# Gate of a mixture-of-experts layer: from steps of two tiles to steps of four

## The chip, the cores and the metric

One core of a Trainium2 chip runs the whole program. The metric is the device time of one execution in microseconds. Engines are called as in the profile: PE is TensorE, DVE VectorE, ACT ScalarE, POOL GpSimd, SP the engine that issues most transfers.

## The reference

A graph network on 6250 nodes of 256 features is followed by a feed-forward layer with eight experts. The change concerns only the second part, cut here to what matters:

```python
H = gelu(xf @ W1 + b1, approximate=False)        # 6250 x 256 -> 6250 x 1024
probs = softmax(H @ Wg + bg)                     # 8 experts
assign = argmax(probs, axis=-1)
for e in range(8):
    y = H @ Wd[e] + bd[e]
    out += where(assign == e, probs[:, e] * y, 0)
out = x + out
```

The result must be close to single precision, so every factor is held as two 16-bit parts, high and low, and a product is made of three or two products of parts.

## The kernel before, in words

The last two stages are `gate` and `experts`, each a block that all engines enter and leave together. A tile is 128 rows (tokens); there are 49, the last one partly filled.

`gate` takes two tiles a step (25 steps, the last with one tile). Its `steps` (L1985) writes steps 0 to 3 out, runs 4 to 21 as nine rounds of a loop of two steps, and writes 22 to 24 out. One step:

- POOL copies the two tiles into `stage` (L2037), a ring of two.
- PE transposes them into one PSUM bank, `TBANK` (L1850, four instructions). The bank is used for every pair, so `pe_transpose` waits (`u.xt`, L1847) until DVE has read the pair before out of it.
- ACT copies the bank to `xt_hi` (L1875), and DVE subtracts that from the bank into `xt_lo` (L1907).
- PE multiplies by `W1` (L1864): the 1024 hidden columns are eight chunks of 128, and a chunk takes six products with 256 columns (two tiles) into one of four PSUM banks.
- For each chunk ACT applies gelu (`hf`, L1893). For five chunks of eight ACT also makes the high part `h_hi` (L1888), for chunks 1, 4 and 6 DVE does (L1920). DVE makes the low part `h_lo` of all (L1925). `hf` holds all eight chunks of a step.
- PE makes the gate's logits from `h_hi` and `h_lo` (`logits`, L2057, 16 products of 16 columns per tile), one step later.
- DVE chooses the expert of every token (`choose`, L2119 to L2139, nine small instructions in a chain, two steps later); PE counts the rank of each token within its expert (`ranks`, L2066 to L2071); DVE turns rank into a place in `sorted_rows` (`place`, L2141 to L2153, five small instructions in a chain, four steps later); POOL scatters the rows there (L2042), one indirect transfer per tile, six steps after their staging.

The order on each engine is the order of the code. Of a two-tile step DVE runs `place` behind the `h_lo` of chunk 0, and behind the `h_lo` of chunk 3 first `xt_lo` of the next step and then `choose`. PE transposes the next two tiles behind chunk 1, counts ranks behind chunk 4, and makes the logits of the step before behind chunk 7:

```python
between[1] = lambda: transpose(i + 1, 1 - par, nxt)
between[4] = lambda: ranks(pe, i - 3, 1 - par, 2, n)
pe_hidden(pe, m, u, i, par, 1 if n == NPAIR else 2, between)
logits(pe, i - 1, 1 - par, 2)
```

After the last `place`, DVE computes the table of tiles for `experts` (L2171 to L2200). SP loads the down weights `wd` and the bias table `bd` (L2000, L2002) at the start of `gate`. `experts` takes 28 pairs of sorted tiles through the same hidden products (`pe_hidden`, `act_hidden`, `dve_hidden`), multiplies by the expert's `wd` (L2276) and scatters the rows to `out`. SP issues its row loads (L2230) one pair after the other, four pairs ahead.

Of the kernel before, what the change touches and what calls it, by code (L numbers as in the profile page):

```python
# [1797 lines left out]
def ffn(nc, m, a):  # L1798
    m.wd = m.at("wd", m.wd_at, [P, NEXP, KH // 2, 2, 2, C], F16)
    take = Place(m, m.ff_at + 8192)  # L1800
    m.xt_hi, m.xt_lo = take("xt_hi", [P, 2, KC, 2 * P], F16), take("xt_lo", [P, 2, KC, 2 * P], F16)
    m.hf = take("hf", [P, KH, 2 * P], F32)
    m.h_hi, m.h_lo = take("h16_hi", [P, 2, KH, 2 * P], F16), take("h16_lo", [P, 2, KH, 2 * P], F16)
    assert take.next <= m.ring_at
    m.hidden = hidden_semaphores(m, "hid")
    gate(nc, m, a)
    experts(nc, m, a)
# [6 lines left out]
UB = 4  # L1814
DVE_HIGH = (1, 4, 6)
# [134 lines left out]
def gate(nc, m, a):  # L1950
# [6 lines left out]
    lg, mx = take("lg", [P, NT + 1, NEXP], F32), take("mx", [P, 2], F32)  # L1957
    now = take("now", [P, 2, NEXP], F32)
    sc, best = take("sc", [P, 2, NEXP], F32), take("best", [P, 2], F32)
    oh, ohf = take("oh", [P, 2, 2, NEXP], F16), take("ohf", [P, 2, 2, NEXP], F32)  # L1960
    rk, slotf, slot = take("rk", [P, 2, NEXP], F32), take("slotf", [P, 2], F32), take("slot", [P, NT], I32)
# [7 lines left out]
    tq, tw = (m.hf[0:1, 2 * q:2 * q + 2, :].rearrange("a k n -> a (k n)").rearrange("a (e t) -> a e t", t=64) for q in range(2))  # L1969
    m.probs = take("probs", [P, NT], F32)  # L1970
    m.bd = m.at("bdB", m.ring_at, [P, NEXP, C], F32)
    u = m.hidden
# [6 lines left out]
    m.s_bd, m.s_prob = S("j_bd"), s_store  # L1979
    m.s_wd = S("i_wd")  # L1980
    NPAIR = NT // 2
    LB, RB = (5, 7), 6
    tiles = lambda i: 1 if i == NPAIR else 2

    def steps(eng, step):  # L1985

        for i in range(4):
            step(eng, i, i % 2, i)
        with eng.Fori(2, NPAIR // 2 - 1) as k:
            step(eng, 2 * k, 0, None)  # L1990
            step(eng, 2 * k + 1, 1, None)
        for i in range(NPAIR - 2, NPAIR + 1):
            step(eng, i, i % 2, i)

    with nc.Block() as block:
        @block.sync
        def _(sp):
            for e in range(0, NEXP, 2):
                n = KH // 2
                sp.dma_start(m.wd[:, e:e + 2, :, :, :, :].rearrange("p e k h t c -> p (e k) (h t c)"),  # L2000
                             m.wd_dram[e * n:(e + 2) * n, :, :].rearrange("n p f -> p n f")).then_inc(m.s_wd, 16)
            sp.dma_start(m.bd[:, :, :].rearrange("p e c -> p (e c)"), bass.AP(a.fbd.tensor, 0, [[0, P], [1, NEXP * C]])).then_inc(m.s_bd, 16)  # L2002
            sp.wait_ge(s_const, 8)
            sp.dma_start(m.sorted_rows[NEXP * REG:NEXP * REG + P, :], prow[:, :]).then_inc(s_padded, 16)
            sp.wait_ge(s_pads, 1)
            for e in range(NEXP):
                at = sp.value_load(padi[0:1, e:e + 1], min_val=e * REG, max_val=e * REG + NP_)
                sp.dma_start(m.sorted_rows[bass.ds(at, P), :], prow[:, :]).then_inc(s_padded, 16)
            sp.wait_ge(s_probS, 1)
            sp.dma_start(m.prob_dram.rearrange("(t p) c -> t (p c)", p=P), probT[:, :]).then_inc(m.s_prob, 16)  # L2010
            sp.wait_ge(s_padded, 16 * (NEXP + 1))

        @block.gpsimd
        def _(pool):
# [16 lines left out]
            LATE = 6  # L2031
            for i in range(NPAIR + 1 + LATE):
                if i <= NPAIR:
                    n = tiles(i)
                    if i >= 2:
                        pool.wait_ge(u.tr, i - 1)
                    pool.tensor_copy(stage[:, i % 2, 0:n, :], rows[:, 2 * i:2 * i + n, 0:C]).then_inc(s_stage, 1)  # L2037
                if i >= LATE:
                    pool.wait_ge(s_slot, i - LATE + 1)
                    for t in range(2 * (i - LATE), 2 * (i - LATE) + tiles(i - LATE)):  # L2040
# [6 lines left out]
        def _(pe):  # L2047
            pe_ahead(pe, u)
            pe.wait_ge(s_const, 8)

            def logits(pe, i, par, ntile):
                pe.wait_ge(u.split, i * KH + 2 * KH)
                pe.wait_ge(s_lgfree, i + 1)
                for j in range(ntile):
                    for n, h in enumerate((m.h_hi, m.h_lo)):
# [17 lines left out]

            def transpose(i, par, ntile):
                pe.wait_ge(s_stage, i + 1)
                pe_transpose(pe, m, u, i, lambda j, k: stage[:, par, j, k * P:(k + 1) * P], ntile)

            def step(pe, i, par, n):
                nxt = 0 if n == NPAIR else 1 if n == NPAIR - 1 else 2

                between = {}
                if nxt:
                    between[1] = lambda: transpose(i + 1, 1 - par, nxt)
                if n is None or n >= 3:
# [14 lines left out]
        def _(act):  # L2099
            act.sem_inc(u.gelu, UB)  # L2100
            act_xt(act, m, u, 0, 0, 2)

            def step(act, i, par, n):
                nxt = 0 if n == NPAIR else 1 if n == NPAIR - 1 else 2
                act_hidden(act, m, u, i, par, 1 if n == NPAIR else 2, nxt)
            steps(act, step)
            act.wait_ge(s_oh, NPAIR + 1)
            act.activation(lg[:, 0:NT, :], lg[:, 0:NT, :], ACT.Exp).then_inc(s_ex, 1)

        @block.vector  # L2110
        def _(dve):
            link = chain_on(m, dve)
            dve_ahead(dve, u)
            dve.sem_inc(s_lgfree, 2)
            link(dve.memset(ones16[:, :], 1.0))
            dve.wait_ge(s_const, 8)

            def choose(dve, i, par, ntile):
# [14 lines left out]
                dve.tensor_copy(lg[:, bass.ds(2 * i, ntile), :], l)  # L2133
# [7 lines left out]
            def place(dve, i, par, ntile):  # L2141
# [9 lines left out]
                lk(dve.tensor_tensor(run[:, :], run[:, :], m.ps[:, RB, 2 * NEXP:3 * NEXP], ALU.add), 3)  # L2151
                lk(dve.tensor_reduce(slotf[:, t], rk[:, t, :], AX.X, ALU.add), 4)
                dve.tensor_copy(slot[:, bass.ds(2 * i, ntile)], slotf[:, t]).then_inc(s_slot, 1)  # L2153

            def step(dve, i, par, n):
                nxt = 0 if n == NPAIR else 1 if n == NPAIR - 1 else 2

                between = {}
                if n is None or n >= 4:
                    between[0] = lambda: place(dve, i - 4, par, 2)  # L2160
                if n is None or n >= 2:
                    between[3] = lambda: choose(dve, i - 2, par, 2)
                dve_hidden(dve, m, u, i, par, 1 if n == NPAIR else 2, nxt, between)
            dve_xt(dve, m, u, 0, 0, 2)
            steps(dve, step)
            for i in range(NPAIR - 3, NPAIR + 1):
                place(dve, i, i % 2, tiles(i))
                if i < NPAIR - 1:
                    choose(dve, i + 2, i % 2, tiles(i + 2))
# [27 lines left out]
            link(dve.tensor_reduce(m.probs[:, :], lg[:, 0:NT, :], AX.X, ALU.add))  # L2197
# [5 lines left out]
def experts(nc, m, a):  # L2203
# [6 lines left out]
    bd = m.bd  # L2210
    y = take("y", [P, 2, 2, C], F32)
    assert take.next <= m.ff_at
    u = m.hidden
    u.first = -(-NT // 2)
    S = m.sem
    s_bd, s_y, s_out, s_used = m.s_bd, S("j_y"), S("j_out"), S("j_used")
# [7 lines left out]
    with nc.Block() as block:  # L2224
        @block.sync
        def _(sp):
# [34 lines left out]
        def _(pe):  # L2261
            def transpose(i, par, q, uses):
# [37 lines left out]
        def _(act):  # L2300
# [7 lines left out]

            act_xt(act, m, u, 0, 0, 2)
# [11 lines left out]
        def _(dve):  # L2321
            dve.sem_inc(s_y, 2)
            dve.sem_inc(s_out, 2)
            dve.wait_ge(s_bd, 16)
# [16 lines left out]
            dve_hidden(dve, m, u, 0, 0, 2, 2)  # L2341
            with dve.Fori(0, (NPAIR - 2) // 2) as k:
# [33 lines left out]
```

## Time and profile before

| | us |
|---|---|
| median of 3 runs | 1857.0 (1855.56 to 1859.79) |
| the profiled execution, its own time | 1859.56 |
| its span | 1857.8 |
| `gate`: first transpose to last slot | 1298.57 to 1511.61 |
| `experts`: first transpose to the end | 1528.68 to 1857.8 |

Over the span PE is busy 85%, DVE 63%, ACT 52%, POOL 50%; the granted clock of PE is 0.97 of full speed on average. These are averages over stages with different limits; `gate` is some 11% of the span. In a timeline row the first number is the start, the second the time from the first start to the last end of merged instructions, `x` their count, and brackets give the engine's idle time before and what ended it.

### The profile page before, as it was taken

What the parts mean: (1) busy time and instruction counts of PE and PEld (TensorE: products, weight loads), DVE (VectorE), ACT (ScalarE), POOL (GpSimd) and SP (SyncE); (2) the same over time, 40 slices, a digit from 0 to 9 for tenths busy, and PEclk for the clock granted to TensorE, in tenths of its full rate; (3) what the DMA queues carried; (4) which work ended last, traced back from release to release, by engine and by line L of the source; (5) the groups of instructions that cost most, each with busy time, mean ns of one, the idle gap of its engine ahead of it and who ended that gap; (6) DMA issues with size and microseconds to landing.
All of it is one profiled execution on the core that took longest, in us unless ns stands there. A gap on an engine that the chain in (4) does not pass through costs nothing. (4 is left out here: it accounts for less than half of the span.)

```text
span 1857.8 us, 36775 instructions
## 1 busy us (share of the span) xinstructions
PE 1579.0 (85%) x11153; PEld 1182.1 (64%) x11154; DVE 1178.6 (63%) x4511; ACT 971.2 (52%) x2001; POOL 936.2 (50%) x989
## 2 busy tenths in 40 slices
PE   0229999999999896989999999975888839999996
PEld 0215666666666696856656555655777728899995
DVE  6478888888886377932234344337788965656663
ACT  0555555555554355832334222228888837766773
POOL 5747677777777000047777777723133332333433
PEclk9999999999999897999999999989999969999998
DMA  8546566666666000478999999837500021111110
GB/s 248 164 138 214 193 208 208 209 208 208 209 208 208 12 0 32 148 260 309 299 314 313 336 321 313 291 122 231 195 34 34 32 75 33 48 47 46 48 47 15
DMA packets 152562, 305.72 MB, mean 165 GB/s; under 512 B 26099, under 2 KB 107989, under 8 KB 144638
## 3 DMA queue, kind: packets, MB, share of 16 engines
q1 hardware_dynamic: 104354, 191.99, 29.6%
q0 software_dynamic: 41744, 105.90, 18.1%
q10 hardware_dynamic: 6348, 6.40, 1.1%
q8 instruction: 58, 0.95, 0.2%
q14 instruction: 58, 0.48, 0.1%
HBM read 212.02 MB, written 99.68 MB: 168 GB/s over the span
## 5 line engine op out<-in xcount | busy, mean ns | idle before, releaser
L1165 POOL DMA_INDIRECT grows<-table_dram,gsrc x680 | 657.9, 967 | 337.3 <-issue 309.0
L1099 PE MATMUL ps<-table,adj 128*128 128x512 f16 x2842 | 707.1, 381 | 5.7 <-PEq L1466 5.7
L1099 PEld LDWEIGHTS ps<-table,adj 128*128 128x128 f16 x2842 | 389.7, 142 | 169.3 <-issue 12.1
L856 ACT ACTIVATE adj<-ps 128x490 f16<-128x490 f32 (+1 forms) x390 | 223.5, 573 | 182.3 <-PE ps L841 178.2
L1893 ACT ACTIVATE hf<-ps,b1f,unscale 128x256 f32<-128x256 f32 (+1 forms) x424 | 233.4, 562 | 119.6 <-PE ps L1864 95.8
L1864 PE MATMUL ps<-xt_hi,fw_parts 128*128 128x256 f16 (+1 forms) x1696 | 255.4, 274 | 5.5 <-DVE xt_lo L1907 5.3
L828 DVE TENSOR_SCALAR oh_k<-iota_k,keyrem 128x246 f16<-128x246 f16 x780 | 237.8, 309 | 0.0
L1925 DVE SCALAR_TENSOR_TENSOR h_lo<-hf,beta,h_hi 128x256 f16<-128x256 f32 (+1 forms) x424 | 190.1, 482 | 70.0 <-ACT h_hi L1888 64.3
L827 DVE TENSOR_SCALAR oh_r<-iota_r,keyrem 128x128 f16<-128x128 f16 x780 | 214.9, 278 | 26.6 <-PE ps L841 21.6
L1048 PE MATMUL ps<-grows,oh_g 128*128 128x512 f16 x680 | 167.1, 380 | 18.0 <-DMA grows<-table_dram,gsrc 18.0
L1864 PEld LDWEIGHTS ps<-xt_hi,fw_parts 128*128 128x128 f16 x1696 | 162.4, 98 | 26.2 <-DVE xt_lo L1907 5.4
L841 PE MATMUL ps<-oh_k,oh_r 128*128 128x245 f16 x780 | 148.7, 273 | 17.3 <-DVE oh_k L828 13.6
L1864 PE MATMUL ps<-xt_lo,fw_parts 128*128 128x256 f16 (+1 forms) x848 | 162.3, 273 | 0.0
L2276 PE MATMUL ps<-wd,h_hi 128*128 x896 | 148.4, 273 | 0.9 <-DVE y L2333 0.9
L841 PEld LDWEIGHTS ps<-oh_k,oh_r 128*128 128x128 f16 x780 | 75.6, 98 | 94.8 <-DVE oh_k L828 20.2
L1888 ACT ACTIVATE h_hi<-hf,beta 128x256 f16<-128x256 f32 (+1 forms) x265 | 133.0, 502 | 1.7
L920 DVE SCALAR_TENSOR_TENSOR tmp_d<-ps,disP,tmp_d 128x256 f32<-128x256 f32 x30 | 14.5, 484 | 186.6 <-ACT tmp_d L1124 186.6
L913 DVE TENSOR_SCALAR oh_g<-iota_r,gloc 128x128 f16<-128x128 f16 x680 | 125.7, 281 | 0.3
L1048 PEld LDWEIGHTS ps<-grows,oh_g 128*128 128x128 f16 x680 | 65.4, 98 | 93.3 <-DMA grows<-table_dram,gsrc 23.9
L2255 POOL DMA_INDIRECT out<-out_rows,in_rows x56 | 57.3, 1023 | 130.3 <-DVE out_rows L2337 121.8
L2276 PE MATMUL ps<-wd,h_lo 128*128 x448 | 122.1, 273 | 0.0
L2042 POOL DMA_INDIRECT sorted_rows<-rows,slot x49 | 48.5, 989 | 128.6 <-DVE slot L2153 121.0
(354 smaller groups left out, 2228.8 us busy)
## 6 DMA issues: line engine op xcount, KB each, us to landing
adj_dram<-adj SPq DMA_DIRECT2D x30, 1568.0 KB
adj<-adj_dram SPq DMA_DIRECT2D x30, 1568.0 KB, 8.2
cv_raw<-fwd SPq DMA_DIRECT2D x64, 256.0 KB, 5.5
table_dram<-table SPq DMA_DIRECT2D x14, 896.0 KB, 4.1
grows<-table_dram,gsrc POOLq DMA_INDIRECT x680
wd_dram<-cv_parts SPq DMA_DIRECT2D x32, 256.0 KB, 5.1
wd<-wd_dram SPq DMA_DIRECT2D x4, 2048.0 KB, 16.8
in_rows<-sorted_rows SPq DMA_DIRECT2D x56, 129.5 KB, 2.1
```

The source lines that it names most:

```text
L827: dve.tensor_scalar(a.oh_r[:, n % OHR, i, :], m.iota_r[:, :], m.keyrem[:, 1, j, w:w + 1], None, ALU.is_equal)
L828: last = dve.tensor_scalar(a.oh_k[:, n % OHR, i, :], m.iota_k[:, :], m.keyrem[:, 0, j, w:w + 1], None, ALU.is_equal)
L841: last = pe.matmul(m.ps[:, n % 3, at:at + keys], a.oh_r[:, n % OHR, i, :], a.oh_k[:, n % OHR, i, 0:keys], start=True, stop=True)
L856: act.activation(m.adj[:, q % 3, d0:d0 + wide, :].rearrange("r d c -> r (d c)"), m.ps[:, n % 3, 0:wide * NT], ACT.Copy).then_inc(a.s_adj, 1)
L1048: last = pe.matmul(acc, m.oh_g[:, n % GOR, j, :], m.grows[:, n % GR, j, :], start=False, stop=part == PT - 1 and j == PARTS[part] - 1)
L1099: last = pe.matmul(acc, adj[:, :, c], table[:, c, :], start=c == 0, stop=c == NT - 1)
L1165: pool.indirect_dma_start(m.grows[:, n % GR, j, :], None, m.table_dram, bass.IndirectOffsetOnAxis(ap=m.gsrc[:, g, part * BT + j:part * BT ...
L1864: last = pe.matmul(m.ps[:, h % UB, 0:n], m.w1[:, 2 * k + half, w, at:at + P], x[:, par, k, 0:n], start=q == 0 and k == 0, stop=q == 2 and ...
L1888: act.activation(m.h_hi[:, par, h, 0:n], m.hf[:, h, 0:n], ACT.Copy, scale=m.beta[:, h:h + 1]).then_inc(u.hi, 1)
L1893: act.activation(m.hf[:, h, 0:n], m.ps[:, h % UB, 0:n], ACT.Gelu, bias=m.b1f[:, h:h + 1], scale=m.unscale[:, 0:1]).then_inc(u.gelu, 1)
L1925: dve.scalar_tensor_tensor(m.h_lo[:, par, h, 0:n], m.hf[:, h, 0:n], m.beta[:, h:h + 1], m.h_hi[:, par, h, 0:n], ALU.mult, ALU.subtract).th ...
L2276: last = pe.matmul(m.ps[:, DB + j, 0:C], h[:, par, k, j * P:(j + 1) * P], w, start=q == 0 and k == 0, stop=q == 2 and k == KH - 1)
```

## The change

`gate` takes four tiles a step (`QT = 4`), 13 steps, the last with one tile: steps 0 to 3 are written out, 4 to 9 are three rounds of a loop of two, 10 to 12 are written out. The hidden products, gelu, `h_hi` and `h_lo` are 512 columns wide. `hf` becomes a ring of four chunks (`HFR = 4`), and gelu of chunk h waits for the `h_lo` of chunk h-4. `choose`, `ranks` and `place` work on four tiles; `ranks` of four tiles takes 14 products. Transposing stays in pairs through the one bank `TBANK`: two pairs for the next step, one behind chunk 1, one behind chunk 4 on PE; ACT and DVE read them behind chunks 2 and 5. On DVE `place` stands behind chunk 0, now for three steps before, and `choose` behind chunk 1, for two steps before. `ranks` stands behind chunk 7, before `logits`. POOL scatters eight pairs after staging (before: six). `experts` keeps its pairs and gets its own buffers and semaphores; the load of `bd` moves from the start of `gate` to `experts`, behind the loads of the first pair of rows.

```diff
+QT, HFR = 4, 4
...
-            sp.dma_start(m.bd[:, :, :].rearrange("p e c -> p (e c)"), bass.AP(a.fbd.tensor, 0, [[0, P], [1, NEXP * C]])).then_inc(m.s_bd, 16)
...
-            LATE = 6
+            LATE = 8
...
+            def transpose(p, par, ntile):
+                pe.wait_ge(s_stage, p + 1)
+                pe.wait_ge(u.xt, p + 1)
+                for j in range(ntile):
+                    for k in range(KC):
+                        last = pe.transpose(m.ps[:, TBANK, k * 2 * P + j * P:k * 2 * P + (j + 1) * P],
+                                            stage[:, par, j, k * P:(k + 1) * P], m.id32[:, :])
+                last.then_inc(u.tr, 1)
+
+            def hidden(i, par, n, between):
+                wide = (QT if n is None else tiles(n)) * P
+                for h in range(KH):
+                    if h == 0:
+                        pe.wait_ge(u.xt, i * 2 + (3 if n is None else 1 + -(-tiles(n) // 2)))
+                    pe.wait_ge(u.gelu, i * KH + (h + 1))
...
+                            last = pe.matmul(m.ps[:, h % UB, 0:wide], m.w1[:, 2 * k + half, w, at:at + P], x[:, par, k, 0:wide],
+                                             start=q == 0 and k == 0, stop=q == 2 and k == KC - 1)
...
             def step(pe, i, par, n):
                 between = {}
+                for half in range(to_come(n)):
+                    ntile = 2 if n is None else min(2, tiles(n + 1) - 2 * half)
+                    between[1 + 3 * half] = lambda half=half, ntile=ntile: transpose(2 * i + (2 + half), half, ntile)
+                hidden(i, par, n, between)
+                if n is None or n >= 2:
+                    ranks(i - 2, par, QT, n)
                 if n is None or n >= 1:
+                    logits(i - 1, 1 - par, QT)
...
+                    act.wait_ge(u.up, i * KH + (h + 1 + 2 * KH))
+                    act.wait_ge(u.split, i * KH + (h + 1))
...
+                    if h in (2, 5) and (h - 2) // 3 < to_come(n):
+                        half = (h - 2) // 3
+                        xt_low(2 * i + (2 + half), 1 - par, half, 2 if n is None else min(2, tiles(n + 1) - 2 * half))
+                    if h == 0 and (n is None or n >= 3):
+                        place(dve, i - 3, 1 - par, QT)
+                    if h == 1 and (n is None or n >= 2):
+                        choose(dve, i - 2, par, QT)
...
             for i in range(RB4):
                 load(i, i)
+                if i == 0:
+                    sp.dma_start(bd[:, :, :].rearrange("p e c -> p (e c)"), bass.AP(a.fbd.tensor, 0, [[0, P], [1, NEXP * C]])).then_inc(s_bd, 16)
```

DVE before, in the written-out step 3 (`h_lo` of chunks 1 to 3, the lowering of the next pair, `choose` of step 1, chunk 4's `h_hi`; `place` joins from step 4 on):

```order
L1925 SCALAR_TENSOR_TENSOR h_lo<-hf,beta,h_hi 128x256 x3
L1907 TENSOR_TENSOR xt_lo<-ps,xt_hi 128x512
L2128 SCALAR_TENSOR_TENSOR now<-ps,inv_g,bgB 128x16
L2129 SCALAR_TENSOR_TENSOR now<-ps,inv_g,now 128x16
L2130 TENSOR_REDUCE mx<-now 128x2
L2131 TENSOR_TENSOR now<-now,mx 128x16
L2133 COPY lg<-now 128x16
L2134 SCALAR_TENSOR_TENSOR sc<-now,prio 128x16
L2135 TENSOR_REDUCE best<-sc 128x2
L2136 TENSOR_TENSOR ohf<-sc,best 128x16
L2139 CAST oh<-ohf 128x16
L1920 TENSOR_SCALAR h_hi<-hf,beta 128x256
```

DVE now, in the written-out step 3 (the first row is `h_lo` of chunk 1; `place` stands ahead of it, behind chunk 0):

```order
L2229 SCALAR_TENSOR_TENSOR q_h_lo<-q_hf,beta,q_h_hi 128x512
L2191 SCALAR_TENSOR_TENSOR now<-ps,inv_g,bgB 128x32
L2192 SCALAR_TENSOR_TENSOR now<-ps,inv_g,now 128x32
L2193 TENSOR_REDUCE mx<-now 128x4
L2194 TENSOR_TENSOR now<-now,mx 128x32
L2196 COPY lg<-now 128x32
L2197 SCALAR_TENSOR_TENSOR sc<-now,prio 128x32
L2198 TENSOR_REDUCE best<-sc 128x4
L2199 TENSOR_TENSOR ohf<-sc,best 128x32
L2202 CAST oh<-ohf 128x32
L2229 SCALAR_TENSOR_TENSOR q_h_lo<-q_hf,beta,q_h_hi 128x512
L2177 TENSOR_TENSOR q_xt_lo<-ps,q_xt_hi 128x2x256
```

The lowering of the transposed rows, which stood ahead of `choose`, now stands behind it.

PE now, in the same step (`stage` rows are the transposes, one pair each; the three pairs of rows between are chunks 2 to 4):

```order
L2065 MATMUL ps<-id_66,stage 128x128 x4
L2078 MATMUL ps<-q_xt_hi,fw_parts 128x512 x4
L2078 MATMUL ps<-q_xt_lo,fw_parts 128x512 x2
L2078 MATMUL ps<-q_xt_hi,fw_parts 128x512 x4
L2078 MATMUL ps<-q_xt_lo,fw_parts 128x512 x2
L2078 MATMUL ps<-q_xt_hi,fw_parts 128x512 x4
L2078 MATMUL ps<-q_xt_lo,fw_parts 128x512 x2
L2065 MATMUL ps<-id_66,stage 128x128 x4
```

Before, one set of transposes stood in a step of eight chunks; now there are two, three chunks apart.

SP now, at the start of `experts`:

```order
L2310 DMA in_rows<-sorted_rows 128x259
L2315 DMA bdB<-fbd 128x2048
L2309 TENSOR_LOAD tile_row
L2309 ISA x2
L2310 ISA
L2310 DMA in_rows<-sorted_rows 128x259
```

The load of `bd` stands between the rows of the first pair and those of the second.

## Rows read from the trace of the kernel before

**Rows 1.** Stretches: busy us of each engine, its count, PE's clock, DMA

```profile
core 0: us, PE busy (x) PEld busy (x) DVE busy (x) ACT busy (x) POOL busy (x), PEclk, DMA share, GB/s
1400.00:1425.00 25.00, 21.24 (x276) 18.70 (x275) 22.26 (x80) 21.18 (x44) 7.73 (x9) 1.00 0.09 32
1600.00:1625.00 25.00, 25.00 (x231) 22.50 (x230) 15.83 (x38) 18.41 (x40) 9.36 (x10) 1.00 0.17 51
```

**Rows 2.** Waits in 1330 to 1480: us in total, times, longest us

```profile
PE ps L2066 <- DVE slot L2153: 24.8, 18, 1.9
```

**Rows 3.** Timeline of PE, 1394 to 1412

```profile
1394.48 0.17 PE L2066 MATMUL ps<-oh,tri 128*128 128x8 f16 x1 [1.54 <-DVE slot L2153]
...
1402.65 0.60 PE L1864 MATMUL ps<-xt_hi,fw_parts 128*128 128x256 f16 x4
...
1404.61 0.35 PE L2057 MATMUL ps<-wg,h_hi 128*128 128x16 f16 x8
...
1405.42 0.60 PE L1864 MATMUL ps<-xt_hi,fw_parts 128*128 128x256 f16 x4
...
1410.84 0.17 PE L2066 MATMUL ps<-oh,tri 128*128 128x8 f16 x1 [1.54 <-DVE slot L2153]
```

**Rows 4.** Timeline of DVE, 1402 to 1412

```profile
1402.41 0.35 DVE L1920 TENSOR_SCALAR h_hi<-hf,beta 128x256 f16<-128x256 f32 x1
1402.80 1.28 DVE L1925 SCALAR_TENSOR_TENSOR h_lo<-hf,beta,h_hi 128x256 f16<-128x256 f32 x3
1403.99 0.68 DVE L1907 TENSOR_TENSOR xt_lo<-ps,xt_hi 128x512 f16<-128x512 f32 x1
1404.59 0.23 DVE L2128 SCALAR_TENSOR_TENSOR now<-ps,inv_g,bgB 128x16 f32<-128x16 f32 x1
...
1406.83 0.35 DVE L1920 TENSOR_SCALAR h_hi<-hf,beta 128x256 f16<-128x256 f32 x1
...
1409.60 0.17 DVE L2148 TENSOR_TENSOR rk<-ps,run 128x16 f32<-128x16 f32 x1
...
1410.64 0.35 DVE L1920 TENSOR_SCALAR h_hi<-hf,beta 128x256 f16<-128x256 f32 x1
```

**Rows 5.** Groups by form of ACT, whole span: busy us, mean ns

```profile
L1893 ACT ACTIVATE hf<-ps,b1f,unscale 128x256 f32<-128x256 f32 x416 | 230.1, 564 | 117.9 <-PE ps L1864 94.0 <-DVE h_lo L1925 9.4
...
L1667 ACT ACTIVATE agg<-agg,b2c,a 128x512 f32<-128x512 f32 x24 | 17.8, 799 | 6.4 <-DVE b2c L1612 6.4
...
L778 ACT ACTIVATE cv_parts<-cv_raw,w_scale 128x512 f16<-128x512 f32 x4 | 2.6, 709 | 0.0
```

**Rows 6.** Groups by form of DVE, whole span

```profile
L796 DVE SCALAR_TENSOR_TENSOR cv_parts<-cv_raw,w_scale,cv_parts 128x512 f16<-128x512 f32 x4 | 2.8, 748 | 2.4 <-ACT cv_parts L778 2.4
```

**Rows 7.** Timeline of PE in the aggregation stage

```profile
1213.46 7.29 PE L1099 MATMUL ps<-table,adj 128*128 128x512 f16 x33
```

**Rows 8.** Timeline of PE around two waits for a transfer

```profile
968.24 1.92 PE L1048 MATMUL ps<-grows,oh_g 128*128 128x512 f16 x5 [2.16 <-DMA grows<-table_dram,gsrc]
969.95 2.95 PE L1099 MATMUL ps<-table,adj 128*128 128x512 f16 x8
...
1027.74 1.47 PE L1048 MATMUL ps<-grows,oh_g 128*128 128x512 f16 x6 [2.78 <-DMA grows<-table_dram,gsrc]
```

**Rows 9.** Stretch behind the first of these waits, columns as in rows 1

```profile
968.00:972.00 4.00, 3.76 (x10) 1.49 (x11) 2.09 (x6) 2.93 (x6) 3.09 (x4) 0.58 0.64 174
```

**Rows 10.** Timeline of PE at the start of the gate

```profile
1298.57 1.09 PE L1850 MATMUL ps<-id,stage 128*128 128x128 f32 x4 [9.68 <-POOL stage L2037]
...
1301.17 1.04 PE L1864 MATMUL ps<-xt_hi,fw_parts 128*128 128x256 f16 x4 [1.52 <-DVE xt_lo L1907]
```

**Rows 11.** Timeline of SP: start of the gate, start of the experts

```profile
1307.56 5.35 SPq L2002 DMA_DIRECT2D bdB<-fbd  x1
...
1525.26 4.95 SPq L2230 DMA_DIRECT2D in_rows<-sorted_rows  x5
```

**Rows 12.** Timeline of PE at the start of the experts

```profile
1533.83 1.06 PE L1850 MATMUL ps<-id,in_rows 128*128 128x128 f32 x4
```

More of the change, by code:

```diff
@@ L1799, in ffn @@
     m.wd = m.at("wd", m.wd_at, [P, NEXP, KH // 2, 2, 2, C], F16)
[L1800 to L1805, printed above, removed]
     gate(nc, m, a)
@@ L1968, in gate @@
     tb2 = take("tb2", [1, NEXP], F32)
-    tq, tw = (m.hf[0:1, 2 * q:2 * q + 2, :].rearrange("a k n -> a (k n)").rearrange("a (e t) -> a e t", t=64) for q in range(2))
     m.probs = take("probs", [P, NT], F32)
-    m.bd = m.at("bdB", m.ring_at, [P, NEXP, C], F32)
-    u = m.hidden
+    take = Place(m, m.ff_at + 8192)
+    xt_hi, xt_lo = take("q_xt_hi", [P, 2, KC, QT * P], F16), take("q_xt_lo", [P, 2, KC, QT * P], F16)
+    hf = take("q_hf", [P, HFR, QT * P], F32)
+    h_hi, h_lo = take("q_h16_hi", [P, 2, KH, QT * P], F16), take("q_h16_lo", [P, 2, KH, QT * P], F16)
+    assert take.next <= m.ring_at + 24576
+    tq, tw = (hf[0:1, q, :].rearrange("a (e t) -> a e t", t=64) for q in range(2))
+    u = hidden_semaphores(m, "quad")
     S = m.sem
@@ L2095, in _ @@
+            for i in range(NQ - 2, NQ):
+                ranks(i, i % 2, tiles(i), i)
             pe.wait_ge(s_prob, 1)
@@ L2155, in step @@
             def step(dve, i, par, n):
[L2156 to L2164, printed above, removed]
+                wide = (QT if n is None else tiles(n)) * P
@@ new lines, in step @@
+                highs = 0
+                for h in range(KH):
+                    if h in DVE_HIGH:
+                        dve.wait_ge(u.gelu, i * KH + (h + 1 + UB))
+                        dve.tensor_scalar(h_hi[:, par, h, 0:wide], hf[:, h % HFR, 0:wide], m.beta[:, h:h + 1], None, ALU.mult).then_inc(u.own, 1)
+                        dve.wait_ge(u.own, i * len(DVE_HIGH) + (DVE_HIGH.index(h) + 1))
+                    else:
+                        highs += 1
+                        dve.wait_ge(u.hi, i * (KH - len(DVE_HIGH)) + highs)
+                    dve.scalar_tensor_tensor(h_lo[:, par, h, 0:wide], hf[:, h % HFR, 0:wide], m.beta[:, h:h + 1], h_hi[:, par, h, 0:wide],
+                                             ALU.mult, ALU.subtract).then_inc(u.split, 1)
+                    if h in (2, 5) and (h - 2) // 3 < to_come(n):
+                        half = (h - 2) // 3
+                        xt_low(2 * i + (2 + half), 1 - par, half, 2 if n is None else min(2, tiles(n + 1) - 2 * half))
[3 more added lines that the diff above has]
+                        choose(dve, i - 2, par, QT)
@@ L2165, in _ @@
+            for half in range(2):
+                xt_low(half, 0, half, 2)
             steps(dve, step)
[L2166 to L2169, printed above, removed]
+            for i in range(NQ - 2, NQ):
+                choose(dve, i, i % 2, tiles(i))
+                place(dve, i - 1, (i - 1) % 2, tiles(i - 1))
+            place(dve, NQ - 1, (NQ - 1) % 2, tiles(NQ - 1))
@@ L2209, in experts @@
     pr = take("prob_rows", [P, 2, 2, 1], F32)
-    bd = m.bd
     y = take("y", [P, 2, 2, C], F32)
     assert take.next <= m.ff_at
-    u = m.hidden
-    u.first = -(-NT // 2)
+    take = Place(m, m.ff_at + 8192)
+    m.xt_hi, m.xt_lo = take("xt_hi", [P, 2, KC, 2 * P], F16), take("xt_lo", [P, 2, KC, 2 * P], F16)
+    m.hf = take("hf", [P, KH, 2 * P], F32)
+    m.h_hi, m.h_lo = take("h16_hi", [P, 2, KH, 2 * P], F16), take("h16_lo", [P, 2, KH, 2 * P], F16)
+    bd = take("bdB", [P, NEXP, C], F32)
+    assert take.next <= m.ring_at + 24576
+    u = hidden_semaphores(m, "hid")
     S = m.sem
-    s_bd, s_y, s_out, s_used = m.s_bd, S("j_y"), S("j_out"), S("j_used")
+    s_bd, s_y, s_out, s_used = S("j_bd"), S("j_y"), S("j_out"), S("j_used")
     s_row = [S(f"j_row{q}") for q in range(RB4)]
```

133 lines of the change are left out of this document (82 added, 51 removed).

## The prediction

> **What bounds the kernel now.** I first read the page's slices to find the stage. The gate runs from 1298.6 to 1511.6 and is all that the change touches, but for one transfer. The table of stretches comes next: in the middle of the gate DVE is busy 22.3 us of 25, PE 21.2, ACT 21.2; in the experts PE is busy without a break [rows 1]. Shares so close say little, so I read who waits for whom: PE waits in each of 18 steps for DVE's `slot`, 24.8 us in all [rows 2], and the first rank product comes back every 16.36 us per two steps, that is per four tiles [rows 3]. That is DVE's own work: from start to start `h_lo` takes 0.40 (three in 1.19), `h_hi` 0.39, `xt_lo` 0.60, `choose` 2.24, `place` 1.04 [rows 4]. For four tiles: 16×0.40 + 6×0.39 + 2×0.60 + 2×2.24 + 2×1.04 = 16.5. So DVE bounds the gate, and PE has 1.5 us of idle time in a step.
>
> **The change, engine by engine, for four tiles.** DVE: a 512-wide instruction of `h_lo`'s form takes 748 ns [rows 6], the 256-wide one 0.48 (1.28 less two starts of 0.40) [rows 4], so from start to start 0.40 + 0.27 = 0.67. For a 512-wide `h_hi` no row stands; between 0.39 (no more than now) and 0.66 (growing like `h_lo`) I take the middle, 0.53. `choose` and `place` are chains of small instructions whose price is not their width: 2.24 and 1.04 come once instead of twice, with some 0.1 for 16 more columns each: 2.35 and 1.10. Sum: 8×0.67 + 3×0.53 + 2×0.60 + 2.35 + 1.10 = 11.6, that is 4.9 less.
> PE: 27 products of 512 columns take 7.29 - 1.47 us [rows 7, 8], 0.216 each, a chunk of six 1.30. Three chunks of 256 columns take 1404.61 - 1402.65 = 1.96 now [rows 3], 0.65 each. So width saves PE nothing: 10.4 for eight chunks. Logits: 0.81 for two tiles [rows 3], 1.62 for four, 0.025 a product; 14 rank products 0.36; transposes are 128 columns wide, 8×0.11 = 0.9. Sum 13.3.
> ACT: gelu 0.56 now; a 512-wide activation takes 0.80, and one of `h_hi`'s form 0.71 [rows 5]. With some 0.1 of overlap between neighbours: 8×0.70 + 5×0.61 + 2×0.5 = 9.7.
> POOL: the same 49 scatters; the second pair's staging now stands behind two scatters that wait for `place`, but it is still done about 1 us before PE can use it (2.5 for two scatters and 0.6 for the copy, behind `place`, against `choose`, two `h_lo`, one `h_hi` and `xt_lo`, 4.9 with what is below).
> If these sums decided, a step would cost PE's 13.3. They don't, for a loop runs through all three engines.
>
> **The loop.** There is one bank for transposing, and PE may fill it for the second pair (behind chunk 4) only when DVE has lowered the first pair out of it (behind chunk 2). DVE comes there only after `place` and `choose`; before, the lowering stood ahead of `choose`, and the next transposing a whole step later. Follow it from the moment the second transposing starts:
> PE: transposes 0.44, chunks 5 to 7 3.90, ranks 0.36, logits 1.62, chunks 0 and 1 of the next step 2.60: 8.9.
> Handover to ACT (the last product's end, 0.16, and the signal, 0.1): 0.3.
> ACT: `h_hi` of chunk 0 stands behind gelu of chunk 1: 0.70 + 0.71: 1.4.
> DVE: `h_lo` 0.67, `place` 1.10, `h_hi` 0.53, `h_lo` 0.67, `choose` 2.35, `h_lo` 0.67, `xt_lo` 0.68: 6.7; signal 0.1.
> Sum 17.4 us against 16.36 now. PE's wait at its second transposing is 17.4 - 13.3 = 4.1. A step of four tiles costs 1.0 more, though every engine has less or the same to do. It holds for steps 4 to 10: 7×1.0 = **+7**.
>
> **The clock.** Behind an idle time of 2.16 us PE was granted 1.2 GHz: the mean of the next 4 us is 0.58 [rows 9], and 5 and 8 products took 1.92 and 2.95 us [rows 8], where full speed gives 4×0.216+0.39 = 1.25 and 1.90: 1.7 us lost. Behind 2.78 at 1027.74 six products took 1.47, full speed [rows 8]; so between 2.2 and 2.8 it happens or not, and the 1.5 us of the gate now leave 1.00 [rows 1, 3]. A wait of 4.1 is longer than any after which the clock held. The cost per step lies between 0 (it holds) and 3.9 (chunks 5 to 7 wholly at half speed); I take 1.4, somewhat under the 1.7 measured, since a part of the slow stretch can fall into the wait or onto the small products. The chunks behind the wait are on the loop, so it counts whole, in steps 3 to 10: 8×1.4 = **+11**.
> The Trainium skill has the same on its page "TensorE: Matmul & The Clock Gate", section "Why this matters for your kernels": it advises against idle gaps between bursts of products, as they bring the half clock back. By that rule the clock falls in each such step; by the shorter waits of this trace alone it could hold, and the second rival is what is left then. This rule speaks against the change.
>
> **Start, end, `bd`.** At the start the second pair must go through the bank before the first product: one more round of 2.6 us, as from 1298.57 to 1301.17 [rows 10]. In steps 0 to 3 DVE has little or no `choose` and `place` and the wait is short; there the saved DVE time can give this back. I take 0 for both, between -4 and +4. At the end the chain of `choose` and `place` behind the last tile is of fewer pieces: **-2**, between -3 and 0. SP needs 5.35 us to issue `bd` [rows 11]; in the gate nothing waited behind it, now the second pair's row loads do. SP issues rows about 1 us apart from 1525.3 (five in 4.95), so the fourth lands, some 2 us behind its issue, at about 1530.6; with `bd` ahead at 1536. PE wants them at 1533.83 [rows 12], so 2 us late; PE is the bound of the experts [rows 1] and doesn't catch up. Between 0 and 5 with the clock's share, I take **+3**. DVE's wait for `bd` is moved behind the first hidden step and covered.
>
> **Sum:** 7 + 11 + 0 - 2 + 3 = +19 on the profiled execution's 1859.56: 1878.6. That execution lies 2.6 above the median of the runs (1857.0), against which +19 gives 1876. I say **1877**. Own range 1869 to 1886.
>
> **Rivals.**
> 1. *DVE's saving arrives* (faster). The gate is bound by DVE now and loses 4.9 us of it per four tiles, so a step falls to PE's 13.3: 12×(16.36 - 13.3) = 37 less, +3 for `bd`, 1823. The point that decides is whether the first pair is lowered within the 4.3 us that PE needs from chunk 1 to its second transposing (0.44 + 3×1.30); by my loop it takes 8.4. For: rows 2 and 4. Against: the order of the code. Were the path a good 1 us shorter than I say and the clock to hold, the result would be near 1857. The Trainium skill favours this rival on "VectorE: DVE Perf Modes", section on the TRN2 errata: it advises wide tiles since each instruction pays a fixed price. The trace agrees with that for DVE alone (0.67 against 2×0.40), not for the gate by itself. Chance 0.12.
> 2. *The loop binds, the clock holds*: 19 less 11, 1865 to 1868. For: 2.78 us without a fall. Chance 0.18.
> 3. *Worse than that*: all three chunks behind the wait are slow in most steps, 8×3 instead of 8×1.4: 1890. Against: the measured 1.7. Chance 0.12.
> 4. *The terms cancel*, 1857 within 4. Chance 0.04.
> My forecast keeps 0.54. That the change doesn't widen the work is excluded by the order of instructions, which shows 128x512 on all three engines.
>
> **Numbers.** 0.2% of this time, about 3.7 us, is what a measurement can tell from no change. Slower: 0.54 + 0.18 + 0.12 = 0.84; same 0.04; faster 0.12. The range 1860 to 1890 holds the forecast, rival 2 and the lower half of rival 3, about 0.8.
>
> **What would show it.** In the profile of the changed kernel: a wait of about 4 us of PE at the second transposes for DVE's `xt_lo`, once per step; PE's clock under 1.00 in the gate, about 0.8 to 0.9, with products of a chunk behind the wait about twice as slow; a period of 18 to 19 us per step; DVE busy less than 70% of the gate; second transposes of the experts some 2 us later behind the start than 5.2. I am wrong if PE is busy throughout the gate, if its wait is under 3 us, if the clock stays 1.00, or if another wait (ACT's for the ring of `hf`, PE's for ranks or logits) is the long one.

## The result and the profile after

| | us |
|---|---|
| before, median of 4 runs | 1857.2 (1855.56 to 1859.79) |
| changed, median of 4 runs | 1893.2 (1888.94 to 1895.41) |
| ratio, 95% interval | 1.0183 (1.0165 to 1.0202) |
| profiled execution of the changed kernel, and its span | 1895.41, 1893.5 |
| `gate`: first transpose to last slot | 1302.07 to 1542.77 |
| `experts`: first transpose to the end | 1564.76 to 1893.5 |

The change costs 36 us, where 19 were forecast; 1893 is outside the range of 1860 to 1890. The stretches that answer to [rows 1], with the same columns:

```profile
core 0: us, PE busy (x) PEld busy (x) DVE busy (x) ACT busy (x) POOL busy (x), PEclk, DMA share, GB/s
1400.00:1425.00 25.00, 16.71 (x138) 9.20 (x139) 15.97 (x39) 11.09 (x17) 9.55 (x11) 0.81 0.11 38
1600.00:1625.00 25.00, 25.00 (x231) 22.55 (x230) 15.61 (x38) 18.01 (x39) 9.79 (x10) 1.00 0.15 44
```

The experts are as before. In the gate no engine is busy for more than some two thirds of the stretch, and PE's clock, 1.00 before, is 0.81. The waits of 1345 to 1480 (us in total, times, longest), which answer to [rows 2], have the pair of names that the forecast's loop asked for:

```profile
ACT q_hf L2149 <- PE ps L2078: 57.1, 29, 6.7
DVE q_h_lo L2229 <- ACT q_h_hi L2144: 50.0, 14, 5.0
PE ps L2065 <- DVE q_xt_lo L2177: 28.4, 7, 4.4
ACT q_hf L2149 <- DVE q_h_lo L2229: 7.2, 4, 1.8
```

Each engine waits for the one before it round the loop: ACT for PE, DVE for ACT, PE for DVE. The ring of four `hf` is the last line: 7.2 us against the 57.1 that ACT waits for PE. PE's timeline over one step, which answers to [rows 3]:

```profile
1424.32 1.09 PE L2065 MATMUL ps<-id,stage 128*128 128x128 f32 x4 [4.41 <-DVE q_xt_lo L2177]
1425.19 1.91 PE L2078 MATMUL ps<-q_xt_hi,fw_parts 128*128 128x512 f16 x4
1426.90 1.06 PE L2078 MATMUL ps<-q_xt_lo,fw_parts 128*128 128x512 f16 x2
...
1429.86 1.03 PE L2078 MATMUL ps<-q_xt_hi,fw_parts 128*128 128x512 f16 x4
1430.73 0.59 PE L2078 MATMUL ps<-q_xt_lo,fw_parts 128*128 128x512 f16 x2
...
1444.62 1.09 PE L2065 MATMUL ps<-id,stage 128*128 128x128 f32 x4 [4.41 <-DVE q_xt_lo L2177]
```

A step takes 20.3 us. Behind the wait of 4.41 four products take 1.91 us; in the last chunk they take 1.03. The stretches of one step show the same in the clock, 1.2 GHz for 6.8 us, 2.4 GHz for 13.6:

```profile
1422.40:1429.20 6.80, 4.88 (x14) 2.37 (x15) 4.07 (x8) 1.12 (x2) 2.79 (x3) 0.51 0.11 39
1429.20:1442.80 13.60, 11.00 (x122) 6.06 (x119) 7.84 (x21) 9.03 (x14) 2.83 (x4) 0.99 0.05 20
```

**Where the 35.7 us of span went**, by the starts of the same transposes in both traces:

| stretch | before | changed | difference |
|---|---|---|---|
| up to the gate's first transpose | 1298.6 | 1302.1 | +3.5 |
| from there to the transposing of pair 10 | 75.4 | 73.4 | -2.0 |
| from there to pair 24 (seven steps) | 114.3 | 141.9 | +27.7 |
| from there to the last slot | 23.3 | 25.4 | +2.0 |
| last slot to the experts' first transpose | 17.1 | 22.0 | +4.9 |
| experts | 329.1 | 328.7 | -0.4 |

The first line is code that the change doesn't touch; in a second profile of the changed kernel (below) the gate began at 1299.6, so it is scatter between executions. The other lines are the change. Seven steps cost 4.0 us more each, where 2.4 were forecast (1.0 for the loop, 1.4 for the clock), and 4.9 us lie behind the gate, where the forecast had a gain. The experiments ask three things: is it this loop, is the clock's part an effect of the idle time, and what is late behind the gate.

### The profile page after: what moved, and what is told of

Same layout as the page of the kernel before. It is cut to its first block and busy times, and to the rows that moved or that the text cites. A ratio compares the mean times of both kernels' runs of the same rounds, so it can differ in the third digit from the quotient of the medians.

```text
span 1893.5 us, 34507 instructions
## 1 busy us (share of the span) xinstructions
PE 1596.6 (84%) x10625; PEld 1136.3 (60%) x10626; DVE 1142.1 (60%) x4211; ACT 930.2 (49%) x1845; POOL 941.4 (50%) x989
## 5 line engine op out<-in xcount | busy, mean ns | idle before, releaser
L1888 ACT ACTIVATE hf<-ps,b1f,unscale 128x256 f32<-128x256 f32 x224 | 123.0, 565 | 87.5 <-PE ps L1859 80.1
L841 PE MATMUL ps<-oh_k,oh_r 128*128 128x245 f16 x780 | 148.6, 273 | 17.4 <-DVE oh_k L828 13.7
L1920 DVE SCALAR_TENSOR_TENSOR h_lo<-hf,beta,h_hi 128x256 f16<-128x256 f32 x224 | 103.8, 484 | 58.7 <-ACT h_hi L1883 55.6
L1859 PE MATMUL ps<-xt_hi,fw_parts 128*128 128x256 f16 x896 | 136.2, 275 | 2.4 <-DVE xt_lo L1902 2.4
L841 PEld LDWEIGHTS ps<-oh_k,oh_r 128*128 128x128 f16 x780 | 75.6, 98 | 94.9 <-DVE oh_k L828 20.3
L2149 ACT ACTIVATE q_hf<-ps,b1f,unscale 128x512 f32<-128x512 f32 (+1 forms) x104 | 78.1, 752 | 100.9 <-PE ps L2078 89.9
L2229 DVE SCALAR_TENSOR_TENSOR q_h_lo<-q_hf,beta,q_h_hi 128x512 f16<-128x512 f32 (+1 forms) x104 | 75.1, 735 | 85.5 <-ACT q_h_hi L2144 84.2
L2078 PE MATMUL ps<-q_xt_hi,fw_parts 128*128 128x512 f16 (+1 forms) x416 | 115.0, 404 | 3.1 <-DVE q_xt_lo L2177 3.0
```

Of the source, the lines that this page charges most:

```text
L841: last = pe.matmul(m.ps[:, n % 3, at:at + keys], a.oh_r[:, n % OHR, i, :], a.oh_k[:, n % OHR, i, 0:keys], start=True, stop=True)
L1859: last = pe.matmul(m.ps[:, h % UB, 0:n], m.w1[:, 2 * k + half, w, at:at + P], x[:, par, k, 0:n], start=q == 0 and k == 0, stop=q == 2 and ...
L1888: act.activation(m.hf[:, h, 0:n], m.ps[:, h % UB, 0:n], ACT.Gelu, bias=m.b1f[:, h:h + 1], scale=m.unscale[:, 0:1]).then_inc(u.gelu, 1)
L2078: last = pe.matmul(m.ps[:, h % UB, 0:wide], m.w1[:, 2 * k + half, w, at:at + P], x[:, par, k, 0:wide], start=q == 0 and k == 0, stop=q == ...
```

## The experiments

### Is it the one bank and DVE's order?

`e1_choose_behind` puts `choose` behind the lowering of the first pair. POOL's `LATE` goes to 10 with it, so that staging stands ahead of the scatters that wait for `place`:

```diff
-            LATE = 8
+            LATE = 10
...
-                    if h == 1 and (n is None or n >= 2):
+                    if h == 2 and (n is None or n >= 2):
                         choose(dve, i - 2, par, QT)
```

> The changed kernel with choose on DVE behind the first pair's xt_lo (chunk 2) instead of ahead of it (chunk 1), and POOL's scatters two pairs later (LATE 10) so that the second pair's staging doesn't stand behind the scatters of the same step. Theory (one bank for transposing, filled again only when DVE has lowered the first pair): the loop loses choose's 2.5 us, PE's wait at the second transposing falls from 4.4 to about 1.7, the clock then holds 1.00 in the gate as it did with 1.5 us of idle time before, and a step goes from 20.4 to about 15.0: 8 x 5.4 = 43 less, about 1850. Rival ring (the ring of four hf buffers sets the step): DVE's work is the same and so is the step, 1893. Rival clock alone (the order of DVE's work is worth its 2.5 us, the clock falls anyway): 8 x 2.5 = 20 less, 1873.

Measured: 1854.9 against 1861.2 of before on that chip, ratio 0.9955 (0.994 to 0.997); on the first chip's 1857 that is 1849. PE's waits in 1395 to 1475:

```profile
PE ps L2065 <- DVE q_xt_lo L2177: 8.6, 5, 1.7
```

A step takes 15.2 us (four from 1391.30 to 1452.21), the clock is 1.00 throughout. `LATE` has a share in this that the theory didn't see (shown below); beside the kernel with `LATE` 10 alone, 1880.5 on the same chip, moving `choose` gives 26 us. Both rivals fall, the ring among them: DVE has the same work and ACT the same ring.

`e2_two_banks` leaves DVE's order and gives each half a bank of its own; `choose`'s logits give one up. `LATE` is 10 here too; the lines that only follow from the new banks are left out:

```diff
-    LB, RB = (5, 7), 6
+    LB, RB, TB = (7, 7), 6, (TBANK, 5)
...
-                pe.wait_ge(u.xt, p + 1)
+                pe.wait_ge(u.xt, max(p, 1) if isinstance(p, int) else p)
...
-                pe.wait_ge(s_lgfree, i + 1)
+                pe.wait_ge(s_lgfree, i + 2)
```

> The changed kernel with a bank of its own for each half of the transposing (both steps' logits share one bank in its place), DVE's order untouched, LATE 10 as above. Theory: PE no longer waits at the second transposing; a step is bound by PE's own 13.3 to 14.1 us at full clock: 8 x 6.3 = 50 less, and the first product comes 2.6 us sooner: about 1840. Rival (DVE arrives late whatever the banks are): the wait moves to the next step's chunk 0 and the step stays over 17: above 1870. Rival ring: 1893.

Measured: 1847.5 against 1861.2, ratio 0.9924 (0.9908 to 0.9941). The second transposing never waits. A wait of 1.1 to 1.25 us came at the next step's chunk 0 for the second pair's `xt_lo`:

```profile
1377.23 1.03 PE L2078 MATMUL ps<-q_xt_hi,fw_parts 128*128 128x512 f16 x4 [1.25 <-DVE q_xt_lo L2177]
```

Steps are by turns 14.4 and 16.3 us, since the clock falls in every other one. Beside `LATE` 10 alone that is 33 us less. So the loop through the one bank is the cause: the wait shrinks to 1.7 us by DVE's order alone and is gone with a second bank. The step of 14.1 wasn't reached, as the rival's late lowering is there too, at a smaller price.

### LATE alone: a surprise

`e4_late10` has the one line `LATE = 10` and was meant as a control.

> The changed kernel with LATE 10 instead of 8 alone, the control for the two kernels that have it too. Theory: in the changed kernel the second pair's staging is ready before PE can use it, so nothing changes: 1893 within 3, wait at the second transposing 4.4 as before. Rival (the staging behind two scatters is what PE waits for): the wait falls by 1 us or more, 8 us or more less.

Measured: 1880.5 against 1861.2, ratio 1.0103 (1.0086 to 1.012). The expectation was wrong: 0.8% of time, some 15 us, hangs on when POOL copies a pair. The rival was nearer in its number, but not in its mechanism: in the changed kernel the copy (1441.78, 0.62 us) ends 2.2 us ahead of the transposes that need it (1444.62). DVE in the changed kernel:

```profile
1441.14 0.66 DVE L2194 TENSOR_TENSOR now<-now,mx 128x32 f32<-128x32 f32 x1
1442.06 0.39 DVE L2196 COPY lg<-now 128x32 f32 x1 [0.26 <-DVE now L2194]
```

and POOL in the same step:

```profile
1440.81 0.97 POOL L2050 DMA_INDIRECT sorted_rows<-rows,slot  x1 [0.30 <-issue]
1441.78 0.62 POOL L2045 COPY stage<-rows 128x512 f32<-128x512 f32 x1
```

With `LATE` 10 a scatter runs there too, but the next copy begins 3.2 us or more behind the subtraction, and DVE's timeline has:

```profile
1417.32 0.19 DVE L2194 TENSOR_TENSOR now<-now,mx 128x32 f32<-128x32 f32 x1
1417.76 0.18 DVE L2196 COPY lg<-now 128x32 f32 x1 [0.25 <-DVE now L2194]
```

In four traces (the changed kernel twice, the two-bank kernel, the best one below) the subtraction takes 0.59 to 0.68 in the 26 steps in which the copy follows directly behind a scatter and begins as the subtraction ends, and 0.19 in all others. The copy by itself doesn't do it. In `e1_choose_behind` it begins in the last 0.05 us of the subtraction in eight steps, but 0.60 us behind the scatter, and the subtraction takes 0.19 in all eight:

```profile
1407.16 0.19 DVE L2194 TENSOR_TENSOR now<-now,mx 128x32 f32<-128x32 f32 x1
1407.30 0.61 POOL L2045 COPY stage<-rows 128x512 f32<-128x512 f32 x1 [0.60 <-PE ps L2065]
```

So the place of the copy is shown as the cause of the longer `choose`, and why it has to stand right behind a scatter isn't. With the longer copy of `lg` (0.39 for 0.18) it makes 0.67 us in the middle of the loop: from the start of the subtraction to DVE's next `h_lo` are 1.98 us against 1.31. PE's wait falls from 4.41 to 3.74, and behind that the clock falls for one stretch of 3.4 us, if at all, instead of 6.8: steps take 17.1 (1383.99 to 1401.13) to 19.0, 18.25 in the mean. The Trainium skill says on "SBUF — State Buffer", section "SBUF: two separate sides", that VectorE and GpSimd share a pair of ports that one of them locks for a whole instruction. The trace agrees that the two disturb each other; which of them held the lock it doesn't show.

### Is the clock's part due to the idle time?

`e3_fill` gives PE 20 products to make while it waits:

```diff
+                    if h == 4 and (n is None or n >= 3) and 4 in between:
+                        pe.wait_ge(u.gelu, i * KH + 6)
+                        for _ in range(20):
+                            pe.matmul(m.ps[:, 5 % UB, 0:512], m.w1[:, 0, 0, 0:P], xt_hi[:, par, 0, 0:512], start=True, stop=True)
                     if h in between:
```

> The changed kernel with 20 extra products of 512 columns (4.3 us at full clock; their result is overwritten by chunk 5) on PE just ahead of the second transposing, in the time in which it waited 4.4 us. Nothing else moves. Theory (the idle time is what drops the clock): granted clock 1.00 in the middle of the gate, the loop alone is left, a step of about 17.9 instead of 20.4: 8 x 2.5 = 20 less, 1873. Rival (the clock falls for another reason, or it costs nothing since the loop hides it): the clock still shows 0.67 and the time is 1893 or up to 20 more, since slow filling products take 8.6 us.

Measured: 1875.1 against 1861.2, ratio 1.0079 (1.0061 to 1.0096): 1.0% or 19 us under the changed kernel's 1.0183, for more work. Its PE:

```profile
1411.78 4.48 PE L2084 MATMUL ps<-q_xt_hi,fw_parts 128*128 128x512 f16 x20
1416.36 0.63 PE L2065 MATMUL ps<-id,stage 128*128 128x128 f32 x4
1416.82 1.03 PE L2078 MATMUL ps<-q_xt_hi,fw_parts 128*128 128x512 f16 x4
```

The clock is 1.00 from 1347 to 1514, and a step takes 17.8 us. The filling ends just ahead of `xt_lo` (DVE's row is 1415.53, 0.69 us), so the loop still sets the step. That splits the 20.3: 16.3 before, 1.5 for the loop, 2.5 for the clock. The idle time brings the clock down, and its price is on the path.

`e8_fill10` is the same with 10 products.

> The changed kernel with 10 filling products (2.15 us at full clock) instead of 20 ahead of the second transposing: an idle time of about 2.3 us is left. In the changed kernel 1.66 us never brought the clock down and 2.51 did once, for 3.4 us. Theory (the length of the idle time decides, in steps): the clock falls in some steps for 3.4 us, a step between 17.8 and 19, 1875 to 1885. Rival (any idle time of over 2 us costs the whole): 20.4 a step, 1893. Rival (only over 3): as with 20 products, 1875.

It ran on a chip on which every kernel was slow (before took 2125.8, 14% more; in the traces of the changed kernels from there nearly all of that lies ahead of the gate). Measured: 2154.6, ratio 1.0135 (1.0109 to 1.0162). Its gate keeps the engines' usual speeds and can be read. The same idle time, two steps in a row:

```profile
1673.25 0.63 PE L2065 MATMUL ps<-id,stage 128*128 128x128 f32 x4 [2.25 <-DVE q_xt_lo L2181]
1673.71 1.03 PE L2078 MATMUL ps<-q_xt_hi,fw_parts 128*128 128x512 f16 x4
...
1691.21 0.63 PE L2065 MATMUL ps<-id,stage 128*128 128x128 f32 x4 [2.25 <-DVE q_xt_lo L2181]
1691.68 1.51 PE L2078 MATMUL ps<-q_xt_hi,fw_parts 128*128 128x512 f16 x4
```

With 2.25 us idle the clock holds in one step and falls for 3.4 us in the next; steps are by turns 18.0 and 19.5. Together, at this place, directly behind 512-column products: 1.7 us idle never cost anything, 2.25 cost 1.5 in every other step, 3.7 some 1.0 in the mean, 4.4 cost 2.5 in the mean. The length of the wait doesn't decide alone. Behind the first wait of 4.43 the clock was down for only 3.4 us in both traces of the changed kernel (a step of 19.5), and behind one of 3.85 in step 3 it stayed up in the first of them,

```profile
1366.56 0.63 PE L2065 MATMUL ps<-id,stage 128*128 128x128 f32 x4 [3.85 <-DVE q_xt_lo L2177]
```

while it fell for 3.4 us behind the same wait in the second, and for 6.8 us in `f2_tail_again` (below), which is the same kernel up to there. So the price of a wait is a range.

### The last wait: the second pair sooner

`e5_early` adds to the two banks:

```diff
-                    between[1 + 3 * half] = lambda half=half, ntile=ntile: transpose(2 * i + (2 + half), half, ntile)
+                    between[1 + half] = lambda half=half, ntile=ntile: transpose(2 * i + (2 + half), half, ntile)
...
-                    if h in (2, 5) and (h - 2) // 3 < to_come(n):
-                        half = (h - 2) // 3
+                    if h in (2, 3) and h - 2 < to_come(n):
+                        half = h - 2
```

(the second hunk on ACT and on DVE).

> Two banks as in the run with two banks, and the second pair transposed behind chunk 2 and lowered behind chunk 3 (not 4 and 5). Theory: what is left of PE's waiting there is chunk 0 of the next step, 1.1 us for the second pair's xt_lo behind chunk 5's h_lo, and the clock falls every other step behind it; lowering two chunks sooner takes both away, a step is PE's own work, 13.3 to 13.5 us instead of 15.35: 9 x 1.9 = 17 less than 1847, about 1830 where the kernel before takes 1861 (ratio 0.983). Rival (DVE's total of 11.6 plus the small instructions' excess is what bounds it): a step stays over 14.5, 1840 or more.

Measured on the slow chip: 2099.3 against 2125.8, ratio 0.9864 (0.9832 to 0.9895). It ran again on a chip of the usual speed, beside the changed kernel:

> The changed kernel itself once more, so that the three beside it have it on the same chip. Ratio to before 1.0183 as measured at first; gate 240.7 us from first transposing to last slot, 22.0 from there to the experts' first transposing.

> [...] Theory: step 13.3, gate about 177 us, 22.0 behind it, ratio 0.983. Rival (DVE bounds a step): ratio 0.987 or more.

Measured: before 1862.8; the changed kernel 1897.2, ratio 1.0191 (1.0161 to 1.0222); this one 1826.8, ratio 0.9814 (0.9784 to 0.9843). Its gate:

```profile
1400.00:1425.00 25.00, 25.00 (x261) 14.30 (x259) 21.05 (x50) 18.77 (x28) 10.35 (x12) 1.00 0.12 42
```

PE is busy without a break, a step takes 13.2 to 13.4 us (1396.70 to 1410.06 to 1423.27), which is the 13.3 of PE's own work in the forecast, and the gate 176 us instead of 241, and 213 before. So four tiles a step beat both kernels by 36 and 70 us once the bank is out of the way.

### What is late behind the gate?

The gate's block ends when every engine is there. The queues of POOL and SP at that point (duration in ns, then the start), in the changed kernel:

```profile
L2004 POOLq DRAIN  x1: 4071/4071/4071, 1556.3 to 1556.3; - x1
L2004 SPq DRAIN  x1: 7/7/7, 1556.6 to 1556.6; - x1
```

and in the kernel before:

```profile
L1995 POOLq DRAIN  x1: 4071/4071/4071, 1519.9 to 1519.9; - x1
L1995 SPq DRAIN  x1: 7/7/7, 1524.1 to 1524.1; - x1
```

POOL comes some 5 us behind its last scatter and then drains for 4.07 us. In the changed kernel that is the last arrival, to 1560.4, 3.8 us behind SP; before, it was level with SP's (1524.0 and 1524.1). So POOL accounts for some 3.8 of the 4.9 us; without it SP would be last, 1.3 us later behind the last slot than before. Both times the experts' first transpose follows 14 us behind that scatter's end (1514.7 to 1528.7; 1551.0 to 1564.8). What grew is the time from the last slot to it, 3.1 us before and 8.2 now. Scatters come every 1.28 us, and here `place` gives four tiles at once: the last nine scatters stand behind `place` of quad 10. `e6_tail` does `place` sooner there:

```diff
             for i in range(NQ - 2, NQ):
+                place(dve, i - 1, (i - 1) % 2, tiles(i - 1))
                 choose(dve, i, i % 2, tiles(i))
-                place(dve, i - 1, (i - 1) % 2, tiles(i - 1))
```

> The changed kernel with one thing moved: behind the last step DVE does place of quad 10 ahead of choose of quad 11 (and place 11 ahead of choose 12). Theory (POOL reaches the end of the gate late since the last nine scatters, 1.28 us apart, stand behind place of quad 10, which is done 4 us later than it could be): the gate's last slot comes when it came, but from it to the first transposing of the experts takes 3 us less, 19 instead of 22; total 1890 against 1893 (ratio 1.0165 to before). Rival (the barrier is late for another reason): the 22 us stay.

> The two edits above together (two banks, early second pair, place ahead of choose behind the last step). Theory: the gains add, about 3 us under the kernel without the last one: 1827 where before takes 1861 (ratio 0.9815). Rival: nothing on top, 1830.

Both ran on the slow chip: 2160.5, ratio 1.017 (1.014 to 1.0199), and 2099.2, ratio 0.9882 (0.9856 to 0.9907) beside 0.9864 for the second without the edit. The time behind the last slot did fall, to 17.6 and 17.4 us, but the slot came later; PE paused between the gate's last logits there, for which `choose` now waits at once. Why it paused on that chip isn't shown. Once more on a chip of the usual speed:

> The changed kernel with place ahead of choose behind the last step, once more: on the last chip the 22.0 us behind the last slot fell to 17.55, but the last slot came some 5 us later, as PE's logits of quad 11, which choose now waits for with nothing ahead of it, took 7.5 us with stalls in issue instead of 1.7. Theory: without these stalls the last slot comes no more than 1 us later and the total is 3 to 4 us less than the changed kernel beside it. Rival (the order itself delays the last slot): no gain.

> All edits together once more. Theory: 3 to 4 us less than the run with the early second pair beside it, ratio 0.981. Rival (the order itself delays the last slot): the same as that run, 0.983.

Measured: 1894.6, ratio 1.0178 (1.0152 to 1.0204), beside 1897.2; and 1827.7, ratio 0.9813 (0.9785 to 0.9842), beside 1826.8. Neither difference is outside the scatter of the runs. The traces tell more, if all is counted from the start of quad 9's first scatter, which the edit doesn't touch. The first of the nine scatters then comes 7.8 us behind it in the changed kernel (1530.87):

```profile
1538.70 0.97 POOL L2050 DMA_INDIRECT sorted_rows<-rows,slot  x1 [3.01 <-DVE slot L2216]
```

and 5.9 us behind it with the edit (1531.56):

```profile
1537.42 0.97 POOL L2050 DMA_INDIRECT sorted_rows<-rows,slot  x1 [1.03 <-DVE slot L2216]
```

That is 2 us, and the experts' first transpose comes 32.2 us behind the same point instead of 33.8 in the changed kernel on that chip: 1.6 sooner, though the last slot itself is 0.7 later, since DVE now waits 0.63 us for PE's ranks. In the pair with two banks it is 1.3 sooner. So the experts follow POOL's scatters and not the last slot, as the theory says. The gain of 3 to 4 was too much by half: POOL had waited only 3.01 us there, 1.03 of it is left, and a gain of 1.6 is too small for the runs to show.

## Why the prediction was wrong

The mechanism was right; two terms of the sum failed, and together they are more than the whole miss.

- **The end** failed most: "the chain of `choose` and `place` behind the last tile is of fewer pieces: **-2**". Measured are +2.0 to the last slot and +4.9 behind it, 9 us more than forecast. The forecast followed only the chain of DVE and left the path through POOL out. `place` of four tiles at once releases nine scatters of 1.28 us late, and POOL, level with SP at the end of the gate before, is there 3.8 us after it. The +2.0 ahead of the last slot wasn't taken apart; its cause stays open.
- **The clock** was right in kind and mis-sized, by 6 us: "I take 1.4, somewhat under the 1.7 measured". Forecast 8 × 1.4 = +11, measured 2.5 in the mean of seven steps, +17. The 1.7 was read behind a wait of 2.16; behind 4.4 the clock stays down for 6.8 us in six of the seven steps, a third of the step, with chunks of 2.6 and 2.1 us where 1.30 is full speed (1425.19 to 1427.76 to 1429.86). Rival 3 (all three chunks slow, 1890) was nearer in its total, though two of the three chunks are slow and not all; it was given 0.12 by an argument from the shorter wait.
- **The loop** was right in its place and nearly in its size. PE's wait at the second transposes for `xt_lo` was forecast at 4.1 and is 4.4; without the clock and the copy a step takes 17.1 to 17.3, forecast 17.4. Forecast +7, measured 7 × 1.5 = +10, of which some 4 are POOL's copy lengthening `choose`. The forecast asked of the staging only whether it is ready for PE, and it is, by 2.2 us where about 1 was forecast; that it runs on top of `choose` and slows it wasn't asked.
- **Start:** forecast 0, measured -2. As said, the first product came 5.2 us behind the first transpose instead of 2.6, and the first steps gave it back.
- **`bd`:** forecast +3, measured nothing. The forecast took 5.35 us for its issue from a place where four loads of 2 MB had just been queued ahead of it. Here SP's row is

```profile
1563.03 0.43 SPq L2315 DMA_DIRECT2D bdB<-fbd  x1
```

  and in the gate the transfer that now stands directly behind the four loads has the long issue; before, behind `bd`, it took 0.55 us:

```profile
1310.51 6.15 SPq L2012 DMA_DIRECT2D sorted_rows<-prow  x1
```

  So the long issue goes with the place and not with `bd`. The second pair's transposes in `experts` follow the first's by 5.06 us instead of 5.15.
- **Rivals.** Rival 1 (DVE's saving arrives, 1823) is what the kernel does once the bank is taken away: 1826.8, or 0.9814 × 1857 = 1823. Its step of 13.3 is right; that the total agrees to the microsecond is partly luck, since its sum has 3 us for `bd` that weren't there and nothing for what is late behind the gate. It failed for the changed kernel by the path from chunk 1 to the second transposing, as argued. Rival 2 (the clock holds, 1865 to 1868) is `e3_fill`, 1.0079 × 1857 = 1872, with the copy's 0.67 a step in it.

The terms as measured: 10 (loop) + 17 (clock) - 2 (start) + 2 + 5 (end) + 0 (`bd`) = 32, 13 more than the forecast 19. With the 3.5 us of scatter between executions ahead of the gate they make the 35.7 of span.

## What to carry to other kernels

When steps get wider, look for what didn't: a buffer that is filled twice a step instead of once turns a harmless order of code into a loop through all engines. Read that loop before the sums. Don't price the clock by a shorter wait that happens to stand in the trace; take a range, since waits of one length cost different amounts here. Follow every engine to the barrier, the one that is seldom busy too. The fix was not to undo the wide step but a second bank and an earlier second fill (with `LATE` 10): -1.9% against the kernel before, where the change alone cost +1.8%.

## What the runs showed of the hardware

- Directly behind 512-column products 1.74 us of idle time never brought PE's clock down to 1.2 GHz, and waits of 3.74 to 3.85 us did in some steps and not in others. In the two-bank kernel, where logits of 16 columns stood ahead of the idle time for 1.6 us, 1.23 to 1.25 us did in every other step; the steps between had 1.06 to 1.11 us and kept 2.4 GHz.
- A VectorE subtraction of two SBUF operands took 0.59 to 0.68 us instead of 0.19 when GpSimd's 128x512 copy followed directly behind an indirect scatter and began as the subtraction ended (26 of 26 steps in four traces). It took 0.19 when the copy began there 0.60 us behind the scatter (8 of 8 steps), and under a scatter with no copy behind it.
- POOL's drain at the end of the gate took 4.071 us in each of the fourteen traces.
- SP took 5.35 us to issue a 1 MB load right behind four loads of 2 MB, and 0.43 us for the same load elsewhere; behind the same four loads another, small transfer took 6.15 us.
- The same program took 2126 us on one chip and 1857 to 1863 on the others. This wasn't followed up; the ratios of the three kernels that ran on both sorts agree within 0.7%.
